# Last stage of a three-stage transformer block on one core: the row maximum written negative by its own instruction, the score scale applied where the turned queries are split

## The reference, cut to what matters

```python
qkv = x @ W_qkv.T                                  # x: the layer-normed rows
q, k, v = jnp.split(qkv, 3, axis=-1)
k_shared = jnp.einsum('bth,bthd->btd', indicator, k)
v_shared = jnp.einsum('bth,bthd->btd', gating_top1, v)
q = q.reshape(Bb, Tt, H, hd).transpose(0, 2, 1, 3)
att = jnp.einsum('bhqd,bkd->bhqk', q, k_shared) * (1.0 / math.sqrt(hd))
att = jnp.where(causal[None, None, :, :], att, -jnp.inf)
att = jax.nn.softmax(att, axis=-1)
y = jnp.einsum('bhqk,bkd->bhqd', att, v_shared)
```

## Time and profile before

| | |
|---|---|
| median of 3 runs | 1482.92 us (1481.59 to 1484.98) |
| the profiled execution | 1483.9 us |
| its span, first to last instruction | 1482.1 us |
| mean granted TensorE clock | 0.958 |
| busy share: PE, PEld, DVE, ACT, POOL | 89%, 75%, 55%, 40%, 31% |
| instructions: PE, DVE, ACT, POOL | 8504, 1629, 1777, 696 |
| last stage with steady pairs | from 985 us to the end |

### The profile page before, as it was taken

One profiled execution on the slowest core, in us unless ns is written; L12 is line 12 of the kernel. 1 busy time (PEld: TensorE's weight loads), 2 busy tenths in 40 slices (PEclk: granted clock), 3 DMA queues, 4 the chain that ended last, 5 costly groups with the idle time before them and its releaser, 6 DMA issues. The chain is left out here.

```text
span 1482.1 us, 23784 instructions
## 1 busy us (share of the span) xinstructions
PE 1322.8 (89%) x8504; PEld 1109.5 (75%) x8504; DVE 816.1 (55%) x1629; ACT 595.5 (40%) x1777; POOL 452.5 (31%) x696
## 2 busy tenths in 40 slices
PE   0799999999999995599999998489899998999997
PEld 0678888888888884478888886368788787878775
DVE  8656656655566321455555552345666656566566
ACT  3443333333334221333333321234546556454646
POOL 3555445544554310233333231021221203122121
PEclk9999999999999997799999999599999999999999
DMA  3222222222222225856655411354141423514040
GB/s 147 98 87 93 93 105 88 93 93 100 86 93 93 93 90 177 241 164 171 171 162 162 147 43 44 141 107 93 37 100 36 93 70 62 116 40 101 16 93 30
DMA packets 59525, 150.71 MB, mean 102 GB/s; under 512 B 7696, under 2 KB 24336, under 8 KB 57872
## 3 DMA queue, kind: packets, MB, share of 16 engines
q1 hardware_dynamic: 59408, 149.18, 34.0%
HBM read 67.37 MB, written 56.62 MB: 84 GB/s over the span
## 5 line engine op out<-in xcount | busy, mean ns | idle before, releaser
L724 PE MATMUL psum<-wr_high,x_high 128*128 128x512 f32 x576 | 234.1, 406 | 5.0 <-DVE x_low L541 5.0
L724 PE MATMUL psum<-wr_high,x_low 128*128 128x512 f32 x576 | 228.9, 397 | 0.0
L724 PE MATMUL psum<-wr_low,x_high 128*128 128x512 f32 x576 | 228.3, 396 | 0.0
L1466 ACT ACTIVATE probs<-psum,row_max 128x256 f32<-128x256 f32 (+1 forms) x384 | 165.1, 453 | 107.6 <-issue 75.2
L1716 POOL TENSOR_TENSOR picked_rows<-picked_rows 128x768 f32<-128x768 f32 (+1 forms) x64 | 61.0, 953 | 269.6 <-DVE picked_rows L1600 265.8
L724 PEld LDWEIGHTS psum<-wr_high,x_high 128*128 128x128 f32 x576 | 109.0, 189 | 28.6 <-DVE x_low L541 5.8
L724 PEld LDWEIGHTS psum<-wr_high,x_low 128*128 128x128 f32 x576 | 108.7, 189 | 25.9
L1618 DVE TENSOR_REDUCE row_max<-psum 128x2 f32<-128x512 f32 (+1 forms) x160 | 109.5, 684 | 31.8 <-PE psum L1821 31.8
L724 PEld LDWEIGHTS psum<-wr_low,x_high 128*128 128x128 f32 x576 | 109.1, 189 | 23.4
L937 ACT ACTIVATE square_scratch<-psum 128x128 f32<-128x128 f32 x192 | 50.7, 274 | 185.4 <-PE psum L1130 185.4
L698 PE MATMUL psum<-m,basis 128*128 128x64 f32 x384 | 76.8, 283 | 40.8 <-POOL m L650 40.8
(11 more groups left out here) (200 smaller groups left out, 3027.5 us busy)
## 6 DMA issues: line engine op xcount, KB each, us to landing
qk<-stage SPq DMA_DIRECT2D x24, 512.0 KB, 2.6
v<-stage SPq DMA_DIRECT2D x24, 512.0 KB, 2.6
g<-gate_rows SPq DMA_DIRECT2D x24, 512.0 KB, 2.6
q_stack_t<-q_t_high SPq DMA_DIRECT2D x64, 192.0 KB, 4.2
q_stack_t<-q_t_low SPq DMA_DIRECT2D x64, 192.0 KB, 5.8
qk_rows<-qk SPq DMA_DIRECT2D x16, 512.0 KB, 5.5
v_rows<-v SPq DMA_DIRECT2D x16, 512.0 KB, 6.9
gate_rows_q<-g SPq DMA_DIRECT2D x16, 512.0 KB, 8.9
```

The costliest lines, as they stand in the source:

```text
L724: last = nc.tensor.matmul(psum[:, PB[(6 * u[1] + n) % 4], :], x[:, q, k], ww[:, w, k, :], start=c == 0, stop=c == 3 * KC - 1)
L1466: last = nc.scalar.activation(pr[:, g % 2, c], psum[:, SB[g % 3], c], ACT.Exp, scale=SCALE_F, bias=mx[:, g % 3, 1, x:x + 1], accum_out=dsu ...
```

## The change

The reduction writes the negative of the maximum, in its own instruction (`negate=True`), and raises `s_max`, for which ACT now waits. The TENSOR_SCALAR, DVE's wait for its own reduction and the semaphore `s_neg` are gone, and `row_max` has half the columns. The scale (32 to the power of -1/2) leaves the exponential and goes into the split of the queries: ACT's copy to `q_t_high` multiplies by it, and DVE's subtraction for `q_t_low` becomes a scalar_tensor_tensor that multiplies the PSUM value by it before it subtracts. The same holds for the queries of the first pair, which are split ahead of the steps.

```diff
-    mx = sb("row_max", [P, 3, 2, HB])
+    mx = sb("row_max", [P, 3, HB])
...
-    s_neg = Signal(sem("scores_max_negated"), NS_F)
...
-                nc.scalar.activation(qhi[:, c], psum[:, QTB[c], 0:TP], ACT.Copy).then_inc(q_high.sem, 1)
+                nc.scalar.activation(qhi[:, c], psum[:, QTB[c], 0:TP], ACT.Copy, scale=SCALE_F).then_inc(q_high.sem, 1)
...
-                act.wait_ge(s_neg.sem, s_neg.at(0, g + 1))
+                act.wait_ge(s_max.sem, s_max.at(0, g + 1))
...
-                    last = nc.scalar.activation(pr[:, g % 2, c], psum[:, SB[g % 3], c], ACT.Exp, scale=SCALE_F,
-                                                bias=mx[:, g % 3, 1, x:x + 1], accum_out=dsum[:, t, h:h + 1])
+                    last = nc.scalar.activation(pr[:, g % 2, c], psum[:, SB[g % 3], c], ACT.Exp,
+                                                bias=mx[:, g % 3, x:x + 1], accum_out=dsum[:, t, h:h + 1])
...
-                V.tensor_tensor(qlo[:, c], psum[:, QTB[c], 0:TP], qhi[:, c].bitcast(F32), ALU.subtract
-                                ).then_inc(q_low.sem, 1)
+                V.scalar_tensor_tensor(qlo[:, c], psum[:, QTB[c], 0:TP], SCALE_F, qhi[:, c].bitcast(F32), ALU.mult,
+                                       ALU.subtract).then_inc(q_low.sem, 1)
...
-                V.reduce_max(mx[:, g % 3, 0, 0:nh], psum[:, SB[g % 3], :].rearrange("p (h n) -> p h n", h=nh), AX
-                             ).then_inc(s_max.sem, 1)
-                dve.wait_ge(s_max.sem, s_max.at(0, g + 1))
-                V.tensor_scalar(mx[:, g % 3, 1, 0:nh], mx[:, g % 3, 0, 0:nh], -SCALE_F, None, ALU.mult).then_inc(s_neg.sem, 1)
+                V.reduce_max(mx[:, g % 3, 0:nh], psum[:, SB[g % 3], :].rearrange("p (h n) -> p h n", h=nh), AX,
+                             negate=True).then_inc(s_max.sem, 1)
```

More of the change, by code:

```diff
@@ L1537, in _ @@
             for s in (mean_var, x_low, dve_f, lg_read, lg_less, gate_inv, q_low, k_picked, v_picked, k_stacked,
-                      s_max, s_neg, pt_out_d, inv, y_norm):
+                      s_max, pt_out_d, inv, y_norm):
                 s.prime(dve)
```

## The result

The changed kernel took 1469.15 us, median of 6 runs (1465.15 to 1471.02); the kernel before, run beside it, 1483.79 (6 runs, 1476.81 to 1485.64). The ratio is 0.9904, 95% interval 0.9879 to 0.9929: faster by 1.0%, 14.6 us between the medians (the interval of the ratio comes to 10.5 to 18 us). The forecast was 1470.0, range 1465 to 1477.5. Across the two later sets of comparisons the kernel before had medians of 1481.9 (24 runs) and 1480.4 (17 runs), so the gain is 11 to 15 us, whichever set it is held against. Times of kernels from different sets are therefore best compared by their ratios to the kernel before.

The account below looks back on a forecast made before the run. PE was taken to set the pace, so a shorter DVE queue gains only from PE's idleness. 7.2 + 3.8 + 0.6 + 1.4 = 13.0 us off 1483.9, then 1.0 for the profiled execution, gave 1470 us; range 1465 to 1477.5.

Parts of the forecast that it names:

- the sum: All gains expected from the shorter DVE queue: 7.2 + 3.8 + 0.6 + 1.4 = 13.0 us.
- Point 1: Steps 12 to 13, six pairs: DVE's copy of transposed probabilities comes earlier, PE's whole wait goes; 7.2 us, bounds 1.0 and 7.2.
- Point 2: Pair start, eight times: ACT's run begins 0.48 us sooner, shortening PE's wait for x_low; 3.8 us, bounds 0 and 4.4.
- Point 3: Second x_low wait, in pairs with PE at full clock over the next step: 3 waits x 0.2 = 0.6 us.
- Point 4: Last pair, with no next one to prepare: each of seven two-step rounds gets 0.2 us shorter, 1.4 us.
- its ring: Last pair's two-step rounds: reduction, copy, PE's products, scores, next reduction; all in one chain, so 0.2 us goes through.
- The negated reduction: DVE's row maximum with the sign put on: taken to cost nothing more than the plain 0.69 us; a second pass, 0.68.
- rival C: DVE's negated reduction is slower, and the kernel with it: a second pass gives +9.1 us, 1492; chance 0.04.
- D: No change: negation is an instruction of its own, or PE's other work fills the waits; 1482 to 1483 us; chance 0.04.
- A: Steps 12 to 13: row statistics wait behind POOL's first fold, gaining 1.0 instead of 7.2 us; 1476.2 us; chance 0.12.
- The clock: PE's low-clock stretches in the pairs: counted as nothing; ends kept, 3.6 us lost (1473.6) or 5.7 gained.
- rival B: Only the clock's fall behind the logits is left in every pair: 5.7 us more gain, 1464.3 us; chance 0.1.

Follow-up runs that it names:

- The run with the scale alone: Changed kernel, scale still moved to the queries, but the TENSOR_SCALAR (times -1) and DVE's wait kept for all 20 groups of a pair: 1482.48 us, ratio 0.9998.
- The run with group 14: Changed kernel with the TENSOR_SCALAR back in group 14 alone (8 of 160): 1477.98 us, ratio to the kernel before 0.9966.
- The run with group 0: Changed kernel with the TENSOR_SCALAR back in group 0 alone: 1472.80 us, ratio to the kernel before 0.9942.
- the run of two groups: Changed kernel with the TENSOR_SCALAR kept in 18 of 20 groups; only groups 14 and 0 use the negated reduction: 1472.24 us, ratio to the kernel before 0.9927.
- the version without x_low waits: Changed kernel; ACT copies x_high before the exponentials at n = 1 and 2, DVE's row maximum of n = 2 behind x_low: 1447.38 us, ratio to the kernel before 0.9761.

## Why the prediction was right, point by point

**The terms.** To see them without the clock, pairs at the same clock must be compared. The run with the scale alone, whose code in a pair costs what the kernel before costs, had a pair at 0.97 and even one at 1.00:

```profile
1258.94:1321.38 62.44, 57.69 (x480) 47.94 (x480) 39.81 (x89) 34.36 (x123) 13.22 (x16) 1.00 0.34 77
1321.38:1385.30 63.92, 59.17 (x480) 49.17 (x480) 39.91 (x89) 34.36 (x123) 13.23 (x16) 0.97 0.34 75
```

63.92 against 62.08 is 1.84 us a pair, which is 1.15 (the copy's wait) + 0.48 (the start) + 0.2 (the second x_low). Over five periods that is 9.2 us. The part of the stage ahead of them lost 1.8 (70.97 to 69.17, both at 0.95), the part behind them 2.1 (99.65 to 97.59, both at 0.94). Together 13.1 us; the sum had 13.0.

- *Point 1, steps 12 and 13 (7.2 us).* Right, with its three steps: the block behind the fold, the second maximum (0.17 forecast, 0.19 measured), and the subtraction that slips in ahead of POOL's addition. One reading under it was off: POOL was not still in the one early case of 0.36 us, but in a 128x3 instruction of 0.86 us. The step held all the same, since the subtraction now starts 0.65 us ahead of the 128x512 addition. The run with group 14 shows the third at work in reverse. Six waits are gone; the run took back 8.8 us between medians for 7.2 expected, with four of its five periods at 0.95.
- *Point 2, the pair start (3.8 us).* Right in path and size, though the wait that shrank on PE is the one for y_heads_t and not the one for x_low that it named. Of the 0.48, that wait shows 0.39 (0.71 to 0.32); the remaining 0.1 stands in PE's busy time of a pair at 0.97 (59.17 to 59.06). PE began the scores of group 1 at 1182.48 before and at 1240.90 after; ACT's exponentials of it began at 1184.51 and 1242.45, so 2.03 us later and 1.55: the 0.48 of the prediction. The run with group 0 had 0.45 us a pair at equal clock, and 3.7 between the medians.
- *Point 3 (0.6 us).* Mis-sized. The step that failed is "3 waits x 0.2": I gave it to the pairs in which the wait was seen, those without a fall ahead of the logits. Without that fall all six have it, 0.97 with the TENSOR_SCALARs of the later groups in place (six times in the run of two groups) and 0.77 without, so 1.2 us. Point 1, at equal clock 6 x 1.15 = 6.9, was 0.3 too large, so the sum hardly moved.
- *Point 4, the last pair (1.4 us).* Right in its ring: `values` at 1444.09 and 1446.77, 2.68 us apart instead of 2.89. The 2.1 us behind the last period also hold one more pair start.
- *The negated reduction.* 684 ns before and after (128x2 from 128x512, 128 of them); rival C is out, and so is D, for it is one instruction: DVE has 1469 instead of 1629.

**The rivals.** A, the statistics behind the fold, is refuted by the row at 1223.50. The clock was the term left at nothing, with both ends kept, and it gave something: the five periods before were 324.39 us, 4.8 above five of 63.92; after, 311.99, 1.6 above five of 62.08. So 3.2 us of it is the clock's, part of the way to rival B: four periods of five had only the short fall behind the logits. Against it stand 2.1 us that the first two stages took longer in the profiled execution. That term I had not put down at all: in the ten profiles of this study nearly the same code reached the first scores at times between 985.5 and 991.3 us. These 5.8 us are as much as the spread of the changed kernel's six runs (5.9), and what decides them is not shown here. So the mechanism and the 13.0 are borne out, but that the forecast of 1470.0 lies within 1 us of the median is in part luck: in the profiled executions 3.2 us one way and 2.1 the other nearly cancelled, and the sum held neither.

**What of the clock stays open.** I argued that 0.48 us less idleness ahead of the first fall might remove it. It was gone, but it stayed away, after the first pair, in the run with group 0, which had that idleness again. That whether a pair gets a short, a long or no fall goes with when it begins as much as with what it does fits the profiles, but no run isolates it. The Trainium skill, "TensorE: Matmul & The Clock Gate", Part 1, ties the clock to how busy PE has been. The traces agree only in part: the version without x_low waits has pairs at 1.00 in which PE was idle for 1.1 us, but with the same 1.1 us it also has one at 0.94, and the run with the scale alone has a pair at 1.00 with 4.75 us of idleness.

## What to carry to other kernels

A tiny instruction can be costly by where it stands: here 16 of 160 TENSOR_SCALARs, 0.17 us of work each, stood in the two groups where POOL's first folds run; 14 of them took 0.70 us, and the two groups carried about three quarters of the gain. Look for a form whose duration has two values (here 0.17 and 0.70 us) and for what ends on the other engine when the long one ends; if it can't be dropped, an instruction that doesn't meet the other engine, here a reduction, can be free in the same place. And before an instruction is shortened, ask whether its engine merely does it in the wrong order: moving two copies and a maximum gave 21.8 us without removing a thing, 13.5 of them by the order at equal clock; the rest went with the clock and is not shown to be the edit's.

## What was not expected

- A chain of two blocks: a DVE instruction 0.08 us late for the free memory lost 1.06 us (1.42 against 0.36).
- Pairs of identical work come in steps of about 1.57 us (58.58, 60.15, 61.70, and 62.08, 63.68), one step for each further stretch that the clock spends at its lower level. Single runs of one kernel differ by up to 12 us (1476.70 to 1488.77 for the kernel before), and a change of 0.2% needs many runs. Steps of this size in seven pairs would give such a spread; that they do is shown in no run.
- Logits matmuls, during which PE counts as fully busy, are followed by a fall of the clock in most pairs, yet by none in the two pairs from 1116.53 to 1233.69 above.
